# A fused adaLN layer on one core: first-layer gates and the second batch's transpose through DRAM, the conditioning rows in four groups instead of six

## What is computed

```python
mod = (silu(c) @ wmod).reshape(2, 6, 1, 512)      # c (2, 512), wmod (512, 3072)
sa, ca, ga, sb, cb, gb = (mod[:, i] for i in range(6))
ga = (2 * (ga >= 0) - 1) * max(abs(ga), 0.25)     # gb likewise
h = layernorm(x) * (1 + ca) + sa
x = x + ga * (h @ masked(att_w).T)                # 512x512; a 32x32 block is kept if its mask sums above 0
h = layernorm(x) * (1 + cb) + sb
x = x + gb * ffn(h)                               # ffn: (silu(h@Wg.T*ag) * (h@Wu.T*au)) @ Wd.T * ad, inner 1376
```

## Time and profile before

| | before |
|---|---|
| median of 3 runs | 178.93 us |
| the profiled execution | 178.75 us |
| its span, first to last instruction | 177.0 us |
| granted TensorE clock | 1.000 |
| TensorE (PE) busy | 169.0 us, 95% of the span |
| DVE, ACT, POOL busy | 97.6, 82.2, 29.9 us |
| first matmul of the feed-forward | 52.7 us after the span's start |

### The profile page before, as it was taken

The page is one execution under the profiler, slowest core; times in us unless marked ns, Lnnn a source line. Parts: engine busy times, 40 slices in busy tenths (PEclk is TensorE's granted clock), DMA queues, the critical chain, the costliest instruction groups (busy, mean ns, idle before and its releaser), DMA issues.

```text
span 177.0 us, 2551 instructions
## 1 busy us (share of the span) xinstructions
PE 169.0 (95%) x899; PEld 127.5 (72%) x899; DVE 97.6 (55%) x195; ACT 82.2 (46%) x115; POOL 29.9 (17%) x40
## 2 busy tenths in 40 slices
PE   6789999898999999999999999999999999999992
PEld 6645445363548888788888888888888888888882
DVE  6864812887266998335555764328644124442574
ACT  3023230918998987833664445543345433352200
POOL 1442520194009440000000000005600000000000
PEclk9999999999999999999999999999999999999999
DMA  6999986999956800431300000000500000000014
GB/s 176 359 411 392 419 273 157 419 409 405 398 226 206 275 15 19 103 93 31 122 0 4 2 4 0 4 0 20 219 7 0 4 0 4 2 4 0 4 59 178
DMA packets 12581, 23.99 MB, mean 136 GB/s; under 512 B 2984, under 2 KB 5296, under 8 KB 12048
## 3 DMA queue, kind: packets, MB, share of 16 engines
q1 hardware_dynamic: 11008, 22.23, 35.3%
q10 hardware_dynamic: 1552, 1.46, 2.7%
HBM read 19.48 MB, written 2.10 MB: 122 GB/s over the span
## 4 chain that ended last, share of the span: by engine, by line
PE 76%; DMA 8%; SPq 6%; DVE 4%; issue 2%; ACT 1%; POOL 1%
PE bank L843 45%; PE bank L913 20%; PE bank L813 6%; DMA wffn<-in_w_down 5%; SPq L234 4%; DMA modw<-in_mod_ln 3%; PE bank L899 2%; PE bank L797 2%; DVE bns L518 1%; SPq L243 1%; PE bank L757 1%; DVE wffn L539 1%; SPq L276 1%; POOL rstd L318 0%; DVE xt L744 0%
## 5 line engine op out<-in xcount | busy, mean ns | idle before, releaser
L843 PE MATMUL bank<-ht,whi_gu 128*128 128x512 f32 x352 | 83.3, 390 | 0.0
L843 PEld LDWEIGHTS bank<-ht,whi_gu 128*128 128x128 f32 x352 | 65.5, 188 | 14.0 <-issue 0.6
L647 DVE SCALAR_TENSOR_TENSOR awork<-bank,scal,awork 128x512 f32<-128x512 f32 x22 | 16.5, 750 | 50.0 <-PE bank L843 48.6
L913 PE MATMUL bank<-whi_dn,in_split 128*128 128x512 f32 x148 | 37.1, 390 | 0.0
L478 ACT ACTIVATE awork<-bank,scal 128x512 f32<-128x512 f32 x22 | 15.2, 690 | 43.9 <-PE bank L843 43.8
L813 PE MATMUL bank<-awork,wffn 128*128 128x512 f32 x64 | 31.8, 610 | 0.8 <-ACT maskt L391 0.6
L913 PEld LDWEIGHTS bank<-whi_dn,in_split 128*128 128x128 f32 x148 | 27.7, 188 | 5.7
L425 ACT ACTIVATE whi_gu<-wffn 128x1024 fp32r<-128x1024 f32 x22 | 23.3, 1058 | 7.3 <-PE bank L843 7.3
L418 ACT ACTIVATE junk<-wffn 128x1536 uint8<-128x1536 uint16 x11 | 16.3, 1481 | 4.9 <-DMA wffn<-in_w_down 4.8
L813 PEld LDWEIGHTS bank<-awork,wffn 128*128 128x128 f32 x64 | 10.5, 191 | 9.4 <-issue 6.6
L656 DVE TENSOR_TENSOR in_split<-awork,in_split 128x512 fp32r<-128x512 f32 x21 | 16.5, 786 | 0.7
(11 more groups left out here) (70 smaller groups left out, 108.8 us busy)
## 6 DMA issues: line engine op xcount, KB each, us to landing
wffn<-in_w_gu SPq DMA_DIRECT2D x10, 512.0 KB, 10.0
wffn<-in_w_down SPq DMA_DIRECT2D x10, 256.0 KB, 11.2
xt<-in_x SPq DMA_DIRECT2D x8, 256.0 KB, 6.2
modw<-in_mod_ln SPq DMA_DIRECT2D x4, 512.0 KB, 7.1
modw<-in_mod_gate SPq DMA_DIRECT2D x2, 1024.0 KB, 9.9
modw<-in_mod_ln SPq DMA_DIRECT2D x2, 1024.0 KB, 9.5
maskt<-in_att_mask SPq DMA_DIRECT2D x4, 256.0 KB, 6.3
awork<-in_att_w SPq DMA_DIRECT2D x4, 256.0 KB, 7.2
```

Of the source, the lines that this page charges most:

```text
L647: dve.scalar_tensor_tensor(inner[:, s % 2, :], bank[gu_bank(s, 1)][:, :], scal[:, c, 1:2], silu_g[:, s % 2, :], ALU.mult, ALU.mult).then_i ...
L843: return pe.matmul(bank[gu_bank(s, u)][:, :], w, h, start=(k == 0 and part == 0), stop=(k == KT - 1 and part == 1))
L913: last = pe.matmul(bank[4 + t][:, :], h, w, start=(c == 0 and part == 0), stop=(c == C - 1 and part == 1))
```

## The change

- **Rows in four groups** (`SETS` = 4): part 0 (2 blocks); parts 1 and 2 (4); part 3 and the first gates (6); second layer norm and gates (12). The first three groups go through bank 6, one `columns` transpose each. The last group is multiplied after `linear(1,1,2)` and its `columns` stands after `linear(1,2,0)`; they were after `(1,1,0)` and `(1,1,2)`. `transposes(8)` to `(11)` keep their places.
- **Loads** in another order: layer-norm parts 1 and 2 ahead of mask 1, x of batch 1 ahead of mask 2.
- **`normalise(0)` in halves** of 256 features (8 instructions); `transposes(0)` waits for the first four. `modulate(0)` and `modulate(3)` do token tile 0 by itself first, and `linear(0, k, 0)` for k = 0 and 3 waits for that alone.
- **Batch 1's blocks through DRAM.** The 16 moves go. Each of the 4 tiles of `normalise(1)` is stored at once in the DRAM tensor `turn` (256 KB, in pieces of 512 bytes); after all four have landed, SP issues 4 loads of 256 KB. Half of the second layer norm's first load is issued between, the other half after.
- **First gates through DRAM.** `gate_all` and `copy_gate` go. One transpose (`gate_line_rows(0)`, after `linear(0,3,0)`), a copy of 8x128 on ACT, two stores of 2 KB on ACT's queue, then, behind `modulate(4)` and the stores' landing, one load on ACT's queue that broadcasts 512 KB. `gate_linear` waits for it.
- **Flags** for three groups of chunks, (0,4), (4,7), (7,11), instead of two; one check of a chunk fewer ahead of the steps and one in each of the first six.

The diff, cut to its core:

```diff
-            sp.wait_ge(xn_ok, 2 * TT)
-            for n in range(BY_SYNC):
-                move_first(sp, n)
+            for t in range(TT):
+                sp.wait_ge(xn_ok, XN_FIRST + t + 1)
+                sp.dma_start(turn[:, :, t * P:(t + 1) * P].rearrange("j p n -> p j n"),
+                             xq0[:, :, t * P:(t + 1) * P]).then_inc(d_turn_out, 16)
             sp.wait_ge(rows_done, 2)
-            sp.dma_start(modw[:, 0, :, :], mod_ln2[0]).then_inc(d_ln2[0], 16)
+            load_ln2(0)
+            sp.wait_ge(d_turn_out, 16 * TT)
+            for j in range(GRP):
+                sp.dma_start(xb0[BLK * j:BLK * (j + 1), :, :],
+                             turn[j].rearrange("(i q) n -> q i n", q=BLK)).then_inc(d_turn[j], 16)
+            load_ln2(1)
...
+            copy_rows(0)
+            modulate(0)
+            copy_rows(1)
+            modulate(1)
+            modulate(2)
+            copy_rows(2)
+            modulate(3)
+            act.wait_ge(gate_done, 1)
+            act.activation(first_grow[:, :], bank[6][0:KT * NB, 0:P], ACT.Copy).then_inc(first_grow_ok, 1)
+            act.wait_ge(first_grow_ok, 1)
+            for b in range(NB):
+                act.dma_start(first_line[b], first_grow[b * KT:(b + 1) * KT, :]).then_inc(d_first_line, 16)
             modulate(4)
+            act.wait_ge(d_first_line, 16 * NB)
+            act.wait_ge(msum_ok, KT)
+            act.dma_start(gates[:, 0:NB, :].rearrange("p b n -> p (b n)"),
+                          first_line.rearrange("b k i -> (b k i)").partition_broadcast(P))\
+               .then_inc(d_first_gates, 16)
             modulate(5)
-            copy_gate(0, bank[6])
             modulate(6)
             modulate(7)
-            copy_gate(1, bank[7])
             check_chunk(next(check_at))
-            check_chunk(next(check_at))
-            copy_rows(5)
+            copy_rows(3)
...
-                dve.wait_ge(gate_ok, b + 1)
+                dve.wait_ge(d_first_gates, 16)
...
+                    elif t == 2:
+                        pe.wait_ge(first_grow_ok, 1)
                     else:
-                        pe.wait_ge(gate_ok, t - 1)
+                        pe.wait_ge(gate_m, 1)
...
             between = {
-                (0, 0): [lambda: rows_ln1(1)],
-                (0, 1): [lambda: columns_ln1(1), lambda: transposes(2)],
-                (0, 2): [lambda: mask_blocks(2)],
-                (0, 3): [lambda: rows_ln1(2)],
-                (1, 0): [lambda: columns_ln1(2)],
-                (1, 2): [lambda: transposes(3), lambda: rows_ln1(3)],
-                (1, 3): [lambda: mask_blocks(3)],
-                (2, 0): [lambda: columns_ln1(3)],
-                (2, 1): [gate_rows],
-                (2, 3): [gate_columns],
-                (3, 1): [lambda: gate_first(0)],
-                (3, 2): [lambda: gate_first(1)],
+                (0, 0): [rows_second],
+                (0, 1): [lambda: columns(1), lambda: mask_blocks(1)],
+                (0, 2): [lambda: transposes(2)],
+                (1, 0): [lambda: transposes(3)],
+                (1, 1): [lambda: mask_blocks(2)],
+                (2, 1): [lambda: mask_blocks(3), rows_third],
+                (2, 2): [lambda: columns(2)],
+                (3, 0): [lambda: gate_line_rows(0, bank[6])],
             }
...
-GROUPS = [(0, 5), (5, C)]
+GROUPS = [(0, 4), (4, C - HELD), (C - HELD, C)]
```

More of the change, by code:

```diff
@@ L201, in adaln_block @@
         d_blocks = [sem(f"d_blocks{j}") for j in range(P // BLK)]
-        d_turn = [sem(f"d_turn{i}") for i in range(GRP)]
+        d_turn_out = sem("d_turn_out")
+        d_turn = [sem(f"d_turn{j}") for j in range(GRP)]
         checked = sem("checked")
@@ L462, in _ @@
             check_chunk(next(check_at))
+            modulate(10)
             round_gu(0)
-            modulate(10)
             modulate(11)
@@ L520, in stats, with normalise_half @@
                 dve.bn_aggr(mv[:, q, t, :], bns[:, q, t, :]).then_inc(stats_ok, 1)
+            def normalise_half(half, tiles):
+                cols = slice(half * HALF, (half + 1) * HALF)
+                for t in tiles:
+                    if half == 0 and t % 2 == 0:
+                        dve.wait_ge(rstd_ok, t // 2 + 1)
+                        dve.wait_ge(stats_ok, t + 2)
+                    dve.tensor_scalar(xn[:, t, cols], xt[:, t, cols], mv[:, 0, t, 0:1], rstd[:, 0, t:t + 1],
+                                      ALU.subtract, ALU.mult).then_inc(xn_ok, 1)
             def normalise(q, tiles=range(TT)):
@@ L749, in _, with mod_rows @@
         def _(pe):
[L750 to L755, removed]
+            def mod_rows(blocks, dst):
+                for i, (at, source) in enumerate(blocks):
                     for j in range(KT):
-                        last = pe.matmul(dst[BLK * j:BLK * (j + 1), 0:P], sc[:, j, i * BLK:(i + 1) * BLK],
-                                         sources[i // each](j)[:, i % each * P:(i % each + 1) * P],
-                                         start=(i == 0), stop=(i == BLOCKS[n] - 1))
+                        last = pe.matmul(dst[BLK * j:BLK * (j + 1), 0:P], sc[:, j, at * BLK:(at + 1) * BLK],
+                                         source(j), start=(i == 0), stop=(i == len(blocks) - 1))
@@ L773, in columns_ln1, with modw_block, rows_first @@
[L773 to L776, removed]
+                return lambda j: m[:, (2 * j + v) * P:(2 * j + v + 1) * P]
+            def modw_block(slot, i):
+                return lambda j: modw[:, slot, j, i * P:(i + 1) * P]
+            def rows_first():
+                pe.wait_ge(silu_c, 1)
+                pe.wait_ge(d_ln1[0], 16)
+                mod_rows([(v, ln1_block(0, v)) for v in range(2)], bank[6])
@@ new lines, in rows_last, with columns @@
+            def rows_last():
+                pe.wait_ge(d_ln2[0], 32)
+                pe.wait_ge(d_ln2[1], 16)
+                pe.wait_ge(d_gate[1], 16)
+                pe.wait_ge(att_read, 3)
+                mod_rows([(KT * slot + i, modw_block(slot, i)) for slot in range(3) for i in range(KT)], bank[2])
+            def columns(n):
+                pe.wait_ge(rows_copied, n + 1)
+                if n == SETS - 1:
+                    pe.wait_ge(att_read, 4)
+                else:
+                    pe.wait_ge(keep_ok, [1, 1, KT][n])
+                    if n:
+                        pe.wait_ge(modc_ok, n)
+                dst = bank[3 if n == SETS - 1 else 7]
+                pe.transpose(dst[:, 0:P], rows[:, n % 3, :], ident[:, :]).then_inc(cols_done, 1)
@@ L1044, in _ @@
             for s in range(STEPS):
-                if s == GROUPS[1][0]:
-                    load_flag(1)
+                for g in range(1, len(GROUPS)):
+                    if s == GROUPS[g][0]:
+                        load_flag(g)
                 if s == 0:
@@ L1050, in _ @@
                     gate_up(s)
-                if s == 4:
-                    flag_sum(1)
+                for g in range(1, len(GROUPS)):
+                    if s == GROUPS[g][0] - 1:
+                        flag_sum(g)
                 if LAG <= s < STEPS - HELD + LAG:
```

250 lines of the change are left out of this document (123 added, 127 removed).

## The result

The changed kernel takes 185.35 us, median of four runs, against 178.89 for the kernel before beside it: a ratio of 1.0354, interval 1.0314 to 1.0394. The profiled execution takes 184.96 us, 6.2 more than the 178.75 before.

What follows compares the result with a forecast made beforehand. Bound: the moment TensorE begins the feed-forward, 52.97 us, with gap-free work after it. Vector lane +0.75 and third flag +0.35 gave +1.1 on 178.75, 179.85; with the median 0.18 above that execution, 179.9; range 177.3 to 181.8.

Steps and rivals of the forecast that it cites:

- The vector lane decides: Before the second layer norm's transposes: gates at 37.3 plus 9.1, with signals 46.5, against 45.75 before: +0.75.
- TensorE's savings: Ahead of the feed-forward: 0.8 from gate transposes, 0.2 from `columns`, 0.9 from each of two waits; all hidden.
- The gap of 1 us before the third rows: On TensorE in batch 0: a sign of being right, a wait of about 1 us before the third group of rows.
- The sign that I had set for too low a price of batch 1's trip: On ACT before batch 1's products: `modulate(4)` ending after 33 would show the trip through DRAM priced too low.
- Gates at 37.3: Before the first gated product: broadcast issued at 31.6, taking 5.7, gates there at 37.3 instead of 34.05, 3.25 later.
- Batch 1 lands at 30.0: Batch 1's stores and four loads through DRAM: landed at 30.0, from a range of 29.8 to 33.
- The two small stores in by 30.0 quiet, 31.9 if each waits: The first gates' 2 KB stores on ACT's queue: issued at 28.4 and 28.9, in by 30.0 or 31.9.
- Rival A: Vector lane in time: gates at 34.8, feed-forward 1.85 earlier, 1.5 with the flag, about 177.4; chance 0.28.
- ACT's wait for the stores as free below 3 us: On ACT ahead of `modulate(5)` to `(7)`: TensorE needs one every 3.4 us, so waiting costs nothing below 3 us.
- The broadcast 5.7: The first gates' 512 KB load on ACT's queue: 4.2 quiet plus 1.5 for the full queue, 5.7 us.
- Rival C: Broadcast and loads obstruct each other: broadcast 8 us, gates at 39.7, feed-forward 3.1 later, 182.2; chance 0.12, within slower.
- The flag, +0.35: In the feed-forward steps: the third group's flag product and its load cost 0.12 and 0.23, together +0.35.

Runs made afterwards that it cites:

- Experiment 9: Against the kernel with batch 1 through DRAM and gates by TensorE (181.7 us): SP issues nothing behind batch 1's loads until they have landed; 183.11 us.
- experiment 2: The changed kernel with only batch 1's 16 SBUF to SBUF moves back, the first gates still through DRAM; 186.11 us.
- experiment 6: Against experiment 2: SP issues the remaining weights and chunks only after the first gates' broadcast has landed; 186.53 us (187.60 and 185.46).
- experiment 4: The changed kernel with SP issuing the feed-forward chunk loads only after the first gates' broadcast has landed; 184.25 us, one run.
- experiment 1: The changed kernel with only the first gates spread by TensorE and ACT again, batch 1 still through DRAM; 181.67 us.

## Why the prediction was wrong

The direction held, and so did the lane that decides; the size did not. I said 179.9, at most 181.8, and it is 185.35. The step that failed is the moment at which the gates are there. Of the 5.1 us by which the profiled 184.96 is above my 179.85, 4.7 are the gates.

- *The vector lane decides, 9.1 us from the gates to the transposes, 7.2 to the feed-forward.* Right: 9.1 and 7.4 (51.28 to 58.72). TensorE's savings are hidden, as forecast. Of the signs, these came: a DVE wait for the broadcast, but until 42.1 and not 36.5 to 38; a gap before `transposes(8)` released by `normalise(2)` (1.39 us); one before `linear(1,0,0)`, of 3.92 for 1.4. The gap of 1 us before the third rows did not (0.18), and TensorE was through with batch 0 at 31.0, not 30.2. The sign that I had set for too low a price of batch 1's trip, `modulate(4)` ending after 33, came too: 34.8.
- *Gates at 37.3.* Here it failed: they came at 42.0. Of the 4.7 us, 3.2 are the issue (34.83 for 31.6) and 1.5 the broadcast (7.2 for 5.7).
- *Batch 1 lands at 30.0.* Measured 33.0, the upper end of the range I had worked out. The stores were in at 26.5, within 26.2 to 28.1. The term that I mis-sized is the four loads: 3.1 to 5.2 us each for the 2.0 to 3.3 of the moves, which are a quarter of their size. I took the favourable end of each because pieces would overlap. Experiment 9 shows that nothing behind them is to blame; why they move only 260 GB/s stays open.
- *The two small stores in by 30.0 quiet, 31.9 if each waits.* Measured 34.6, and 35.5 in experiment 2. I had priced their flight with the 1.4 us of a quiet stretch and with ACT's moves; under loads it is over 5. That alone puts the issue this late with batch 1 in time: in experiment 2 `modulate(4)` ended at 31.07, and the issue came at 35.56. Rival A, with its 0.28, needed it at 30.3. I had also counted ACT's wait for the stores as free below 3 us; there it was 4.94 and cost TensorE 2.05.
- *The broadcast 5.7.* Measured 7.2; experiment 6 gives 3.8 with empty engines. The Trainium skill's page "DMA: Bandwidth & Descriptors", section "Queues, rings and completion order", has each DMA engine take turns between queues, from which I estimated 6.0. Beside loads the runs show 7.2, 7.0, 6.7 (experiment 2) and 6.2 (experiment 4), all above it; what makes up the rest, no run shows. The same section says that the increment of a semaphore lands only after every earlier write of that DMA engine, across its queues; stores that took over 5 us among loads and 1.7 and 3.0 without them fit that, but no run here separates it from plain queueing.
- *Rival C, a broadcast of 8 us, gates at 39.7, 182.2.* Nearest in kind, and it got only 0.12, because I let the broadcast alone go wrong. The three prices sit in one chain and all depend on the same full engines; I took each near its favourable end, and the range allowed for one miss, not three.
- *The flag, +0.35.* Right for the flag itself (0.12 and 0.23); 0.45 in all from 58.72 on.
- Left out altogether: that the granted clock can fall when TensorE stands. In the changed kernel it is hidden behind the gates; in experiments 1 and 2 it is not.

## What to carry to other kernels

A round trip through DRAM in place of on-chip work was not worth its price here, and beside a weight stream least of all: the same broadcast cost 3.8 us quiet and 7 beside the stream, and stores of 2 KB took 1.7 to 3.0 and over 5. Whether it pays where the DMA engines are idle, these runs don't say; the four loads of batch 1 took 6.5 us even with nothing beside them. Price each transfer of a chain in the state in which the engines will be, and move all of them to the bad end together when one state governs them. Before counting what a resource is relieved of, find the lane that ends last; here the other lane had 2.6 us of slack, and the detour brought its gates 8.1 us later.

## What the runs showed that I had not expected

- Four loads of 256 KB from DRAM, each to 32 partitions, keep the engines at a share of 1.04 and move 260 GB/s; weight loads to 128 partitions moved 411 at 1.00. That the number of partitions is the reason was not tried.
- Around a standstill of TensorE of 3.92 us the granted clock was 0.50 (1.2 GHz) from about 34.4 to 37.8, and seven products took 1.4 us more. In experiment 2, after 4.64 us, 96 records took 5.35 us for 2.83. In experiment 9, after 3.00 us, three products took 2.84 us at a granted clock of 1.00; in experiment 1, after 3.09 us, it was 0.50 from 35 to 38. Why the one fell and the other did not, no run shows.
- Two delays of 3.2 and 7.6 us gave 6.6 together. They run side by side: in the changed kernel the stores and `modulate(4)` end at nearly the same moment, 34.6 and 34.8 us, and the broadcast waits for both. That the two together cost less than the gates' alone fits the 12 blocks of rows, which took 2.83 us there and 5.35, at the lower clock, in experiment 2.
